# Listing every expert's first 512 rows ahead of its further blocks in a mixture-of-experts kernel

## What is computed

```python
x = x + 0.5 * moe(layernorm(x))      # first block
x = x + gated_heads(layernorm(x))    # 8 heads, scan along the tokens ("mix")
x = x + 0.5 * moe(layernorm(x))      # second block, same weights
x = x + 0.5 * ternary_ffn(layernorm(x))
x = x + linear_attention(layernorm(x))
x = x + 0.5 * ternary_ffn(layernorm(x))

def moe(xf):                         # 8 experts, top 2, hidden 512
    shared = gelu(xf @ Wfc_s + bfc_s) @ Wproj_s + bproj_s
    gate = normalized top-2 of softmax(xf @ Wr)
    routed = sum_e gate[:, e] * (gelu(xf @ Wfc[e] + bfc[e]) @ Wproj[e] + bproj[e])
    return shared + routed
```

## Time and profile before

| | |
|---|---|
| median of 3 runs | 1166.69 us (1166.6 to 1167.32) |
| profiled execution | 1157.41 us, its span 1155.7 us |
| mean granted clock of TensorE | 0.95 of full speed |
| busy | PE 1012.9 us (88%), DVE 818.6 (71%), POOL 643.6 (56%), ACT 639.3 (55%) |
| chain that ended last | PE 48%, POOL 19%, DVE 13%, issue 11%, ACT 6% |

### The profile page before, as it was taken

How to read it: one execution, slowest core, us unless ns; L and a number is a source line. 1 busy time by engine, 2 the same in 40 slices (tenths; PEclk the granted TensorE clock), 3 DMA queues, 4 the chain that set the end, 5 groups by cost and what they waited for, 6 DMA issues and landing times.

```text
span 1155.7 us, 16233 instructions
## 1 busy us (share of the span) xinstructions
PE 1012.9 (88%) x4744; PEld 708.9 (61%) x4744; DVE 818.6 (71%) x2327; ACT 639.3 (55%) x1265; POOL 643.6 (56%) x751
## 2 busy tenths in 40 slices
PE   6788999998979999999978989899976668989996
PEld 5335777765647667667746447777834445656663
DVE  7775886758878787888674775676744678777661
ACT  2335667765565676666543336676744345455543
POOL 4006556447998888877661026555256767663440
PEclk9899999999999999999997899999987889999998
DMA  8577767740000000000002025687710000000000
GB/s 264 193 254 250 226 213 237 255 125 24 17 12 13 14 15 12 15 5 2 1 1 67 7 71 196 214 258 225 218 50 23 24 19 28 14 24 10 10 15 23
DMA packets 63495, 105.26 MB, mean 91 GB/s; under 512 B 7888, under 2 KB 42192, under 8 KB 63376
## 3 DMA queue, kind: packets, MB, share of 16 engines
q1 hardware_dynamic: 54320, 85.60, 22.8%
q0 software_dynamic: 9088, 18.63, 5.6%
HBM read 79.29 MB, written 26.87 MB: 92 GB/s over the span
## 4 chain that ended last, share of the span: by engine, by line
PE 48%; POOL 19%; DVE 13%; issue 11%; ACT 6%; DMA 1%; another core or an unknown queue 1%; POOLq 0%; SPq 0%; ACTq 0%; DVEq 0%
PE bank L208 6%; POOL wr L678 3%; PE bank L457 3%; PE bank L455 3%; PE bank L474 3%; POOL head_rstd L1379 3%; PE bank L456 3%; PE bank L453 3%; PE bank L472 3%; PE bank L473 3%; PE bank L1193 2%; PE bank L1153 2%; PE bank L1159 2%; POOL got L678 2%; PE bank L1199 2%
## 5 line engine op out<-in xcount | busy, mean ns | idle before, releaser
L622 POOL DMA_INDIRECT spare_all<-xs,list_row x156 | 158.0, 1013 | 237.0 <-DVE list_row L786 109.8
L858 DVE TENSOR_TENSOR hid_lo<-hid,hid_hi 128x512 fp32r<-128x512 f32 (+1 forms) x184 | 112.1, 611 | 74.1 <-ACT hid L559 44.7
L558 ACT ACTIVATE hid_hi<-bank,b_up_of 128x512 fp32r<-128x512 f32 (+1 forms) x138 | 86.7, 628 | 56.0 <-PE bank L457 36.8
L559 ACT ACTIVATE hid<-bank,b_up_of 128x512 f32<-128x512 f32 (+1 forms) x184 | 113.0, 624 | 5.0 <-issue 1.7
L678 POOL DMA_INDIRECT got<-ys,y_slots x80 | 85.9, 1074 | 44.6 <-DMA ys<-spare_all 26.0
L1272 ACT ACTIVATE gate_b<-bank,head_rstd 128x128 f32<-128x128 f32 x256 | 73.1, 370 | 63.5 <-POOL head_rstd L1379 63.0
L208 PEld LDWEIGHTS bank<-ident,spare_all 128*128 128x128 f32 x476 | 61.2, 151 | 69.6 <-issue 59.2
L208 PE MATMUL bank<-ident,spare_all 128*128 128x128 f32 x476 | 78.8, 290 | 22.1 <-DVE spare_all L401 15.7
L559 ACT ACTIVATE hid<-bank,cols_sb 128x512 f32<-128x512 f32 x64 | 44.0, 687 | 91.5 <-PE bank L453 79.1
L455 PE MATMUL bank<-xh,wr 128*128 128x512 f32 (+1 forms) x184 | 78.9, 429 | 13.2 <-issue 7.0
L1379 POOL TENSOR_TENSOR head_rstd<-head_var,neg_half 128x4 f32<-128x4 f32 x64 | 75.9, 1186 | 5.3
(11 more groups left out here) (325 smaller groups left out, 2694.2 us busy)
## 6 DMA issues: line engine op xcount, KB each, us to landing
wr<-wq SPq DMA_DIRECT2D x92, 512.0 KB
wq<-wr SPq DMA_DIRECT2D x16, 512.0 KB, 5.7
ys<-spare_all SPq DMA_DIRECT2D x32, 256.0 KB
got<-in_w_mlp SPq DMA_DIRECT2D x8, 512.0 KB, 5.6
xs<-spare_all SPq DMA_DIRECT2D x16, 256.0 KB, 2.3
spare_all<-xs,list_row POOLq DMA_INDIRECT x156
out_x<-X SPq DMA_DIRECT2D x8, 256.0 KB, 2.3
ys<-in_x SPq DMA_DIRECT2D x1, 1920.0 KB
```

Of the source, the lines that this page charges most:

```text
L559: nc.scalar.activation(hid[:, n % HC, 0:w], bank[up_bank(n)][:, 0:w], ACT.Gelu_apprx_tanh, bias=bias).then_inc(s["gelu_done"], 1)
L622: g.indirect_dma_start(out=xin[:, j % XIN, b], out_offset=None, in_=xs, in_offset=bass.IndirectOffsetOnAxis(ap=list_row[:, n:n + 1], axis=0))\
L858: v.tensor_tensor(hid_lo[:, q, 0:w], hid[:, n % HC, 0:w], hid_hi[:, q, 0:w].bitcast(F32), ALU.subtract).then_inc(s["lo_done"], 1)
```

## The change

Three parts, in both blocks.

*The order of the lists.* `find_spots` gives the first full block of each expert the slots from 0 on, and the further full blocks the slots behind. `pairs` (full blocks of an expert) is split in `has_first` (0 or 1) and `further`; two running sums in place of one; a row's place gets a second correction if it lies behind its expert's first block. `find_experts` compares each list's number with 16 ends in place of 8. `find_stores` asks only whether any expert has more rows up to the tile than its first block holds; if none has, the count is up to the last first block, else all stores. The number, width and order of the lists' slots stay.

*The gathers.* `moe_fetch_first` issues all eight parts of tile 0 and four of tile 1 with no wait but `rows_stored`; the constants of the last part, set before it up to now, are set between the two.

*The last two lists, both halves.* ScalarE evicts them (`evict_list`, steps 116 and 120) and copies them to `y_out` (`finish_list`, steps 119 and 121), ahead of the GELUs of those steps. VectorE's loop ends at step 115 with the `finish` of list 20, and the sums of tile 0 follow.

The core of the diff (declarations left out):

```diff
+            def evict_list(k):
+                j = list_of(k)
+                act.wait_ge(*s.at("down_done", (k + 1) * HC))
+                act.wait_ge(*s.at("back_in", k - 1))
+                act.wait_ge(*s.at("lists_out", j))
+                nc.scalar.activation(y_f[k % 2][:, 0:width(j)], bank[3 + k % 2][:, 0:width(j)], ACT.Identity,
+                                     bias=b_dn_of[:, SLOTS[j]:SLOTS[j] + 1]).then_inc(s["lists_out"], 1)
+
+            def finish_list(k):
+                j = list_of(k)
+                act.wait_ge(*s.at("back_in", k + 1))
+                act.wait_ge(*s.at("y_stored", 16 * (j // YOUT), j % YOUT))
+                nc.scalar.copy(y_out[:, j % YOUT, 0:width(j)], bank[5][:, 0:width(j)]).then_inc(s["finished"], 1)
...
+                if c == 0 and list_of(k - 2) in LATE_LISTS:
+                    evict_list(k - 2)
+                if n == LISTS_END + 3:
+                    finish_list(AHEAD + LISTED - 2)
+                if n == LISTS_END + HC + 1:
+                    finish_list(AHEAD + LISTED - 1)
...
-            g.iota(block_starts[:], [[0, 2], [TW, TILES]], base=0, channel_multiplier=0,
-                   allow_small_or_imprecise_dtypes=True).then_inc(const_ready, 1)
...
-        def moe_fetch_first(pool, s, ring):
-            for i, half in ((0, 0), (0, 1), (1, 0)):
-                if (i, half) == (0, 1):
-                    pool.wait_ge(*s.at("up_done", LISTS_END - 1))
-                if (i, half) == (1, 0):
-                    pool.wait_ge(*s.at("down_done", LISTS_END))
-                for n in range(half * TB, half * TB + TB):
-                    moe_fetch(pool, s, i, n, ring)
+        def moe_fetch_first(pool, s, ring, between=lambda: None):
+            for n in range(TOP * TB):
+                moe_fetch(pool, s, 0, n, ring)
+            between()
+            for n in range(TB):
+                moe_fetch(pool, s, 1, n, ring)
...
-                steps.link(v.tensor_tensor_scan(ends[:], every[:, 0:EXPERTS], pairs[:], 0.0, ALU.mult, ALU.add))
-                steps.done(v.tensor_tensor(begins[:], ends[:], pairs[:], ALU.subtract))
+                steps.link(v.tensor_scalar(has_first[:], pairs[:], 1.0, None, ALU.min))
+                steps.done(v.tensor_tensor(further[:], pairs[:], has_first[:], ALU.subtract))
+                steps.link(v.tensor_tensor_scan(first_ends, every[:, 0:EXPERTS], has_first[:], 0.0, ALU.mult, ALU.add))
+                steps.done(v.tensor_tensor_scan(further_ends, every[:, 0:EXPERTS], further[:], first_ends[:, EXPERTS - 1:EXPERTS], ALU.mult, ALU.add))
                 steps.done(v.tensor_tensor_scan(single_ends[:], every[:, 0:EXPERTS], singles[:], 0.0, ALU.mult, ALU.add))
-                steps.done(v.tensor_scalar(paired[:], pairs[:], float(TW), None, ALU.mult))
-                steps.done(v.tensor_scalar(pairs_end[:], ends[:], float(TW), None, ALU.mult))
-
-                steps.link(v.tensor_scalar(past_full[:, 0:1], ends[:, EXPERTS - 1:EXPERTS], float(FULL), None, ALU.max))
+                steps.done(v.tensor_tensor(first_at[:], first_ends, has_first[:], ALU.subtract))
+                steps.done(v.tensor_scalar(first_rows[:], has_first[:], float(TW), None, ALU.mult))
+                steps.link(v.tensor_scalar(first_end[:], first_ends, float(TW), None, ALU.mult))
+
+                steps.done(v.scalar_tensor_tensor(further_off[:], further_ends, -1.0, further[:], ALU.add, ALU.subtract))
+                steps.done(v.scalar_tensor_tensor(pairs_end[:], further_ends, -1.0, has_first[:], ALU.add, ALU.add))
+                steps.link(v.tensor_scalar(past_full[:, 0:1], further_ends[:, EXPERTS - 1:EXPERTS], float(FULL), None, ALU.max))
                 steps.done(v.tensor_scalar(past_full[:, 1:2], past_full[:, 0:1], 2.0, -2.0 * FULL, ALU.mult, ALU.add))
+                steps.done(v.tensor_tensor(further_off[:], further_off[:], first_at[:], ALU.subtract))
+                steps.done(v.tensor_scalar(pairs_end[:], pairs_end[:], float(TW), None, ALU.mult))
...
+                steps.done(v.tensor_scalar(further_off[:], further_off[:], float(TW), None, ALU.mult))
...
+                steps.link(v.tensor_tensor(ranked, place[:], by_expert(first_end[:]), ALU.is_ge))
+                steps.link(v.tensor_tensor(ranked, ranked, by_expert(further_off[:]), ALU.mult))
+                steps.link(v.tensor_tensor(place[:], place[:], ranked, ALU.add))
...
-                steps.link(v.tensor_tensor(past[:], block_no[:], ends[:].unsqueeze(1).broadcast_to(by_block), ALU.is_ge))
-                steps.link(v.tensor_reduce(expert_of[:], past[:], AX_X, ALU.add))
+                steps.link(v.tensor_tensor(past_both[:], block_no[:, :, 0:1].broadcast_to(by_both),
+                                           ends[:].rearrange("p k e -> p (k e)").unsqueeze(1).broadcast_to(by_both), ALU.is_ge))
+                steps.link(v.tensor_reduce(expert_of[:], past_both[:], AX_X, ALU.add))
+                steps.link(v.scalar_tensor_tensor(expert_of[:], past_both[:, :, EXPERTS - 1], -float(EXPERTS), expert_of[:], ALU.mult, ALU.add))
...
-                steps.done(v.tensor_tensor(beyond[:], upto_tile[:], paired[:].unsqueeze(1).broadcast_to([P, SOON, EXPERTS]), ALU.is_gt))
-                steps.link(v.tensor_tensor(begun[:], upto_tile[:, :, EXPERTS - 1:EXPERTS].broadcast_to([P, SOON, TILES]),
-                                           block_starts[:], ALU.is_gt))
-                steps.done(v.tensor_reduce(beyond_any[:], beyond[:], AX_X, ALU.max))
-                steps.link(v.tensor_reduce(blocks_upto[:], begun[:], AX_X, ALU.add))
-                steps.link(v.tensor_scalar(blocks_upto[:], blocks_upto[:], begins[:, EXPERTS - 1:EXPERTS], None, ALU.add))
-                steps.link(v.scalar_tensor_tensor(blocks_upto[:], beyond_any[:], FULL + 1.5, blocks_upto[:], ALU.mult, ALU.max))
+                steps.link(v.tensor_tensor(beyond[:], upto_tile[:], first_rows[:].unsqueeze(1).broadcast_to([P, SOON, EXPERTS]), ALU.is_gt))
+                steps.link(v.tensor_reduce(beyond_any[:], beyond[:], AX_X, ALU.max))
+                steps.link(v.scalar_tensor_tensor(blocks_upto[:], beyond_any[:], FULL + 1.5,
+                                                  first_ends[:, EXPERTS - 1:EXPERTS].broadcast_to([P, SOON]), ALU.mult, ALU.max))
...
-                if c == 3 and 2 <= k <= LAST_LIST + 1:
+                if c == 3 and k >= 2:
                     finish(k - 2)
...
-            for n in range(HC, (LAST_LIST + 2) * HC + 1):
+            for n in range(HC, LISTS_END):
...
-            finish(LAST_LIST)
             sums_next()
...
-            consts()
-            moe_fetch_first(pool, moe, FETCHED_WIDE)
+            moe_fetch_first(pool, moe, FETCHED_WIDE, consts)
```

More of the change, by code:

```diff
@@ L157, in macaron_kernel @@
         zrow = sb("zrow", [P, P])
-        block_starts = sb("block_starts", [P, 2, TILES])
         block_no = sb("block_no", [P, LISTED, EXPERTS])
@@ L249, in macaron_kernel @@
         y_slots = sb("y_slots", [P, TOP, BLOCKS], U32)
-        units, pairs, singles, single_ends, pairs_end, single_off, paired = (sb(k, [P, EXPERTS]) for k in (
-            "units", "pairs", "singles", "single_ends", "pairs_end", "single_off", "paired"))
+        units, pairs, singles, single_ends, pairs_end, single_off, first_rows = (sb(k, [P, EXPERTS]) for k in (
+            "units", "pairs", "singles", "single_ends", "pairs_end", "single_off", "first_rows"))
+        has_first, first_at, further, first_end, further_off = (sb(k, [P, EXPERTS]) for k in (
+            "has_first", "first_at", "further", "first_end", "further_off"))
         past_full = sb("past_full", [P, 2])
@@ L256, in macaron_kernel @@
         beyond_any = sb("beyond_any", [P, 2])
-        ends = sb("ends", [P, EXPERTS])
+        ends = sb("ends", [P, 2, EXPERTS])
+        first_ends, further_ends = ends[:, 0], ends[:, 1]
         SOON = 2
         upto_tile = sb("upto_tile", [P, SOON, EXPERTS])
-        begun = sb("begun", [P, SOON, TILES])
         blocks_upto = sb("blocks_upto", [P, SOON])
@@ L267, in macaron_kernel @@
         stores_of = sb("stores_of", [P, SOON, YOUT], I32)
-        begins = sb("begins", [P, EXPERTS])
-        past = sb("past", [P, LISTED, EXPERTS])
+        past_both = sb("past", [P, LISTED, 2 * EXPERTS])
+        past = past_both[:, :, 0:EXPERTS]
         expert_of = sb("expert_of", [P, LISTED])
@@ L291, in macaron_kernel @@
         LISTS_END = (AHEAD + LISTED) * HC
+        LATE_LISTS = (LISTED - 2, LISTED - 1)
         LAG, SHARED_LAG = HC, HC - 1
@@ L746, in find_spots @@
                 steps.done(v.tensor_tensor(single_off[:], single_off[:], pairs_end[:], ALU.subtract))
+                steps.done(v.tensor_scalar(further_off[:], further_off[:], float(TW), None, ALU.mult))
                 steps.done(v.tensor_copy(upto_tile[:].rearrange("p i e -> p e i"), upto.rearrange("p e (i b) -> p e i b", b=TB)[:, :, 0:SOON, TB - 1]))
                 steps.wait()
```

(19 more changed lines are left out.)

## The result

| | before | changed | ratio, 95% interval |
|---|---|---|---|
| median beside each other | 1165.31 us (10 runs) | 1176.51 us (10 runs, 1171.06 to 1182.71) | 1.0100 (1.0073 to 1.0126) |
| the same pair on a second chip | 1153.51 us (20 runs) | 1167.53 us (5 runs) | 1.0129 (1.0099 to 1.0160) |
| profiled execution, its span | 1157.41, 1155.7 us | 1180.23, 1178.5 us | |
| mean granted clock | 0.95 | 0.947 | |

The forecast was 3.9 us slower; the change costs 11 us (medians of the first chip) to 15 us (ratio on the second). The first view is PoolE's timeline at the first handover of the changed kernel, which answers to the earlier trace rows.

What follows compares the result with a forecast made beforehand. It took uncovered VectorE routing arithmetic and late signals at the handovers, the gather chain being nearly hidden, as the bounds. Cost 4.8 less gain 0.9 is 3.9 us slower: 1166.7 becomes 1170.6 us, range 1162.8 to 1173.7.

Steps and rivals of the forecast that it cites:

- the paragraph on the gathers: Handovers: earlier gathers make tile 0 ready at 250 instead of 261.3, passing no other PoolE work but the last part's constants.
- Late now, on time then: Rival: moving gathers from the last matmuls frees late GELU signals; handovers give 3.2 and 5.5 us, 1162.8 us; chance 0.18.
- GELUs that start late beside ScalarE's new work: Sign at the last lists that would show the forecast wrong; ScalarE's evictions and copies were expected to fit.
- The handovers' term: Both handovers from expert block to the block behind: gain 0.5 + 0.4 = 0.9 us, bounds 0 and 8.7.
- `find_spots`: Routing arithmetic on VectorE: 2.3 us longer in each block, with nothing covering it.
- the first marks: Sign at the start of each block's routing: TensorE would stand some 7.2 and 4.0 us for them.
- The low-clock rival: Second block, behind the wait for marks: one more low-clock stretch costs 1.6 us, 1172.2 us; chance 0.10.
- the main case: Late signals at the handovers in both kernels: 3.9 us slower, 1170.6 us; chance 0.45.
- The limit: Gathers' store wait: experts stay under 512 rows, so 8 blocks suffice; rival otherwise over 1185 us, chance 0.02.
- ScalarE's two evictions and copies at nothing: Last two lists: each 0.4 to 0.5 us, fitting ScalarE's idle time; cost taken 0, bounds 0 and 0.5 a handover.

Runs made afterwards that it cites:

- whole_again: The changed kernel run once more, unaltered, beside the others on the second chip: 1.0129 of the kernel before.
- act_alone: The kernel before with only ScalarE's part of the change (evictions and copies of the last two lists, shorter VectorE loop): 1.0002 of the kernel before.
- order_alone: The kernel before with only the new order of the lists, old gather waits and VectorE's old work kept: 0.9984 of the kernel before.
- gathers_behind: The changed kernel with all twelve gathers held back behind the last up of the lists: 1.0124 of the kernel before.
- four_in_flight: The changed kernel with PoolE waiting until four gathers have landed before issuing four more, again ahead of tile 1's: 0.9961 of the kernel before.
- lists_landed: The kernel before with each list's row gathers waiting until the last list's have landed: 1.0593 of the kernel before.
- plain_for_gathers: The changed kernel with gathers 5 to 12 replaced by plain transfers of the same size from fixed rows: 0.9937 of the kernel before.
- six_then_six: The changed kernel with six gathers, a wait until they have landed, then six more: 0.9977 of the kernel before.
- half_rate: The changed kernel with a 1.04 us PoolE operation behind each of the twelve gathers, starting them every 2.4 us: 1.0079 of the kernel before.
- run 8: The same run as lists_landed: the kernel before with each list's row gathers waiting until the last list's have landed: 1.0593 of the kernel before.

## Why the prediction was wrong

- **The step that failed** is in the paragraph on the gathers: "The twelve gathers pass no other work on PoolE but the last part's constants". It asked what the gathers overtake on PoolE's own queue and priced their new place beside the last lists at nothing, as it did the two waits that it removed. That place cost 12.5 + 7.7 us in the profile after, 11.6 + 4.5 in whole_again, and 0.3 with pauses between groups of four. It was no term of the sum, had no bounds, and so the range had no room for it.
- **A rival had the mechanism by half.** "Late now, on time then" said that the lateness goes with gathers beside the last matmuls, and followed it to the place that they leave, not to the one that they move to. There the ring of the lists stood, which has little slack for a late signal. Its condition came true (the handovers gave 3.4 and 5.7 us, for bounds of 3.2 and 5.5), and the time went the other way. One of the forecast's own signs of being wrong came true too, GELUs that start late beside ScalarE's new work; act_alone shows that this work is not the cause.
- **The handovers' term was mis-sized**: 0.9 us taken for late signals in both kernels, 9.1 measured. The late signals went with the run of twelve gathers that the change moved away; order_alone, with runs of four, gives 8.7 us of it. But a long run does not always do it: in gathers_behind twelve gathers stand beside the same matmuls, and the six at the handover still take 2.74 us. In the term itself the 0.26 us from a matmul's end to the GELU is left out at the second handover (850.7 should be 850.9), which changes it by 0.2 us.
- **`find_spots`: right.** From `singles` to the product with `pick` it took 4.68 us before (40.65 to 45.33); VectorE's timeline of the changed kernel:

```profile
40.46 0.17 DVE L749 SCALAR_TENSOR_TENSOR singles<-pairs,units 128x8 f32<-128x8 f32 x1
...
47.47 0.69 DVE L786 TENSOR_TENSOR gate_b<-pick,place 128x512 f32<-128x512 f32 x1
```

  7.01 us, 2.33 more for 2.3 forecast. TensorE stands 7.23 us and 3.35 + 0.67 = 4.02 us for the first marks, for 7.2 and 4.0.
- **The low-clock rival: true in part, beside the main case.** Behind the longer wait in the second block two matmuls took 2.03 us (675.47 above) which took 1.08 before at the same place, and the shift at the marks grew from 2.3 to 3.4 us. The granted clock over these two was 1.00 before (656.1 to 657.1) and 0.50 after (675.5 to 677.5). The Trainium skill ("TensorE: Matmul & The Clock Gate", Part 1) says that the clock is throttled by default and that activity releases it. The trace agrees as far as it goes: the clock fell behind the longer wait, and at 0.50 it cost 1.1 us.
- **The limit was reached**, as counted: PoolE's wait ends at 240.19, while TensorE is still at the lists, not behind the last store.
- **ScalarE's two evictions and copies at nothing: right** within what 0.3% can tell.

With what the profiles showed, the sum comes near: marks 2.2 + 3.4 = 5.6, handovers −9.1, last lists +16.1 (whole_again) is +12.6 us, measured +14.9 (1.29% of 1153.5); without the last lists −3.5, measured −4.5 (four_in_flight). It does so within 3 us for nine of the eleven kernels that it fits (all but lists_landed), and misses plain_for_gathers and six_then_six by 5 and 7 us. For the profile of the pair itself, with 20.2 us at the last lists, it gives +16.6 where +11.7 was measured. A profile is one execution, and the stalls differ from one to the next.

## What to carry to other kernels

When work is moved away from a place where it does harm, price the same harm at the place that it moves to, first of all where a ring of engines has little slack. Two waits that look like leftovers can be what paces a queue: before they go, ask what ran between them. Gathers issued in groups of four with a pause between them cost next to nothing beside such a ring here (0.3 us), while the unpaced ones made the kernel 11 to 15 us slower; the version that keeps the change and paces the gathers (four_in_flight, or the old waits put back) beats the kernel before by 0.4%, and on the second chip the changed one by 1.7%.

## What the runs showed of the hardware that was not expected

TensorE's signals, and only these, come late while PoolE issues indirect gathers at full pace. Lateness here is the time from the last end of an instruction that updates a semaphore to the recorded update, so it is the least that it can be; some updates have no record. In the first 870 us of all fourteen profiles, counted over the semaphores that one engine alone updates, none of 7476 recorded updates of ScalarE and of 11829 of VectorE comes more than 0.02 us behind; of 13403 of TensorE, 618 come over 1 us behind. In the changed kernel the ten recorded between 244 and 258 us have a median of 6.9 and at most 11.9 us, and seven of them are let go in a burst, at 257.40 to 257.70, some 2.5 us behind the end of the last gather (253.99 + 0.95). For runs of indirect gathers in that time (both blocks, and mix between them), in the twelve profiles other than half_rate and plain_for_gathers, the latest signal from the start of the run to 3 us behind its end; a run is gathers whose starts are at most 1.6 us apart:

| gathers in the run | runs | with a signal over 1 us late | latest |
|---|---|---|---|
| 1 | 585 | 0 | 0.2 us |
| 2 or 3 | 241 | 2 | 1.5 us |
| 4 | 178 | 32 | 4.2 us |
| 6 | 20 | 14 | 4.2 us |
| 8 | 61 | 53 | 5.8 us |
| 12 | 13 | 13 | 11.9 us |
| 5, 7, 10 or 14 | 21 | 15 | 4.8 us |

Beside the last lists and the handovers, the gathers at 2.4 us and the plain transfers of the same size had no signal over 1 us late. The ends of matmuls are modelled in these records, so whether the matmul itself or its signal is held is open; that the readers start late is not. Why gathers do this to TensorE alone was not tried.

Length is not all of it. The two runs of twelve with signals 10.7 and 11.9 us late are the ones beside the last lists, where the DMA engines are busy 0.90 and 0.83 of the time over the first 10 us of the run. In the other eleven the latest is 5.2 us; five of them lie at a handover of before, act_alone or gathers_behind, with the DMA engines busy some 0.3. No run holds a gather run of twelve fixed and changes the load of the DMA engines, so what that load adds to a long run was not separated. The runs within the lists bring signals that are late by 2.8 to 5.5 us at the most in every kernel here but lists_landed (0.9 us), and the one try at them (run 8) cost more.
